# Rearranging the first 80 microseconds of a two-layer graph-attention kernel: wider loads of x, an earlier row of factors, gathers without a gate

## The reference

```
h   = relu(layernorm(x))              # per row
Wh  = h @ W                           # 8192 x 128
e   = leaky_relu(src[:, None] + dst[None, :], 0.2)   # src, dst = Wh @ a[:128], Wh @ a[128:]
att = softmax(where(adj > 0, e, -inf), axis=1)
```

## Time and profile before

| | us |
|---|---|
| runs (3) | 1973.93, 1978.59, 1979.74; median 1978.59 |
| the profiled execution | 1969.02, span of its trace 1967.1 |
| PE busy (span share) | 1906.6 (97%) |
| DVE, ACT, POOL busy | 1740.1 (88%), 1471.5 (75%), 1242.6 (63%) |
| first matmul of tile 0 | 82.13 |
| PE's longest stop after it | 130.55 to 135.67 |

### The profile page before, as it was taken

One profiled execution on the slowest core, in us unless ns is written; L12 is line 12 of the kernel. 1 busy time (PEld: TensorE's weight loads), 2 busy tenths in 40 slices (PEclk: granted clock), 3 DMA queues, 4 the chain that ended last, 5 costly groups with the idle time before them and its releaser, 6 DMA issues.

```text
span 1967.1 us, 39089 instructions
## 1 busy us (share of the span) xinstructions
PE 1906.6 (97%) x16858; PEld 1898.0 (96%) x16858; DVE 1740.1 (88%) x2023; ACT 1471.5 (75%) x1745; POOL 1242.6 (63%) x1010
## 2 busy tenths in 40 slices
PE   4789999999999999999999999999999999999998
PEld 3689999999999999999999999999999999999997
DVE  7888898998989899898969898998989899898985
ACT  4988897888889888898771877777788777778710
POOL 3675776767767575775640777767677676768600
PEclk9799999999999999999999999999999999999999
DMA  8999898899989788897990798888989788888900
GB/s 252 349 344 342 291 320 268 299 328 344 319 287 334 275 304 285 309 328 268 370 361 12 262 365 290 299 306 292 338 285 332 274 300 308 293 329 295 329 19 13
DMA packets 181381, 566.46 MB, mean 288 GB/s; under 512 B 18768, under 2 KB 49872, under 8 KB 179664
## 3 DMA queue, kind: packets, MB, share of 16 engines
q0 software_dynamic: 142848, 520.16, 74.9%
q1 hardware_dynamic: 33424, 41.36, 6.3%
q10 hardware_dynamic: 4928, 2.36, 0.5%
HBM read 548.01 MB, written 15.79 MB: 287 GB/s over the span
## 4 chain that ended last, share of the span: by engine, by line
PE 86%; DMA 5%; DVE 4%; ACT 2%; POOL 1%; issue 1%; SPq 0%; DVEq 0%; POOLq 0%
PE psum L766 84%; DMA arena<-in_adj_dram,piece_rows 4%; ACT arena L360 2%; PE psum L724 1%; DVE arena L1063 1%; POOL arena L350 1%; DVE arena L864 1%; DVE arena L378 1%; DMA arena<-x_mid 1%; PE psum L713 0%; DVE st L839 0%; DMA arena<-in_x_dram 0%; POOL piece_rows L396 0%; PE psum L691 0%; DVE h_all L885 0%
## 5 line engine op out<-in xcount | busy, mean ns | idle before, releaser
L766 PE MATMUL psum<-h_all,arena 128*128 128x129 f32 x16384 | 1841.6, 275 | 10.1 <-DVE arena L1063 10.0
L766 PEld LDWEIGHTS psum<-h_all,arena 128*128 128x128 f32 x16384 | 1836.4, 192 | 13.0 <-DVE arena L1063 10.3
L350 POOL DMA_INDIRECT arena<-in_adj_dram,piece_rows x992 | 1233.2, 1243 | 623.7 <-ACT arena L360 434.0
L360 ACT ACTIVATE arena<-arena,half_step 128x1024 uint8<-128x1024 int32 x992 | 1370.5, 1440 | 287.2 <-DMA arena<-in_adj_dram,piece_rows 156.5
L1063 DVE SCALAR_TENSOR_TENSOR arena<-arena,sd_col 128x1024 f32<-128x1024 f32 x512 | 641.2, 1277 | 103.1 <-PE psum L766 98.4
L1063 DVE SCALAR_TENSOR_TENSOR arena<-arena,rho_col 128x1024 f32<-128x1024 f32 x448 | 563.5, 1278 | 69.3 <-PE psum L766 66.3
L378 DVE STREAM_TRANSPOSE arena<-arena 128x1024 f32<-128x1024 f32 x248 | 306.0, 1235 | 8.7 <-ACT arena L360 8.4
L360 ACT ACTIVATION_READ_ACCUMULATOR arena<-arena,half_step 128x1 f32 x512 | 92.5, 181 | 0.0
L1063 DVE SCALAR_TENSOR_TENSOR arena<-psum,rho_col,arena 128x1024 f32<-128x1024 f32 x64 | 79.1, 1267 | 6.8 <-PE psum L766 6.6
L724 PE MATMUL psum<-W_ext,arena 128*128 128x131 f32 x256 | 38.5, 313 | 13.5 <-DVE h_all L885 10.0
L724 PEld LDWEIGHTS psum<-W_ext,arena 128*128 128x128 f32 x256 | 36.3, 224 | 14.9 <-issue 10.6
(11 more groups left out here) (126 smaller groups left out, 195.1 us busy)
## 6 DMA issues: line engine op xcount, KB each, us to landing
arena<-in_adj_dram,piece_rows POOLq DMA_INDIRECT x992, 5.9
arena<-in_x_dram SPq DMA_DIRECT2D x48, 128.0 KB, 5.8
x_mid<-arena SPq DMA_DIRECT2D x8, 512.0 KB, 6.9
edgesT<-arena SPq DMA_DIRECT2D x4, 1024.0 KB, 9.1
arena<-edgesT SPq DMA_DIRECT2D x4, 1024.0 KB, 16.8
arena<-x_mid SPq DMA_DIRECT2D x8, 512.0 KB, 6.6
out_dram<-arena SPq DMA_DIRECT2D x28, 128.0 KB, 11.3
h_mid<-arena SPq DMA_DIRECT2D x6, 512.0 KB, 3.0
```

The costliest lines, as they stand in the source:

```text
L350: pool.indirect_dma_start(adj_in[n % NA], None, adj_pieces, bass.IndirectOffsetOnAxis(ap=piece_rows[:, column:column + 1], axis=0))\
L360: nc.scalar.activation(pack_bytes[h][:, k, a], adj_in[n % NA], ACT.Sign, bias=half_step[:, 0:1], accum_out=into).then_inc(masked, 1)
L766: last = nc.tensor.matmul(acc_tile(g, k), wTs[m % RING][:, k * P:(k + 1) * P], h_all[:, j, 0:FZ], start=(j == 0 and k % 2 == 0), stop=(j = ...
```

## The change

- x is loaded in 16 DMAs of 256 KB with runs of 4 KB. A partition then holds 8 consecutive rows, and the order that the rest of the kernel wants is restored where the transposed z is copied out of PSUM: four instructions of 128 x 256 with a strided PSUM read replace each one of 128 x 1024.
- Layer 0's exponents are shifted by the maximum over the first eighth of the columns, known after part 0, instead of over all. Highest, lowest and invalid are still computed, within group 0's loop.
- `first_r` (the r of the first 8 tiles) runs on ACT ahead of mask 14; DVE limits it, PE transposes it, and it goes through DRAM to `r_row`; `diagonals` and `spread_r` are gone.
- POOL no longer waits for x.
- The copies of h stand between the normalisings, one part later than before.

```diff
+FIRST_R = 14
             indices(0, 0, G)
-            pool.wait_ge(x_loaded[XP // 2 - 1], 16 * BK)
             for n in range(len(PASSES) * PIECES):
                 load_piece(pool, n)
-                if n == 2:
-                    pool.wait_ge(x_loaded[XP - 1], 16 * BK)
...
-        def load_x(eng, i, which):
-            for q, block in quarters(x, i)[2 * which:2 * which + 2]:
-                eng.dma_start(x_all[q, part_of(0, i), :], block).then_inc(x_loaded[i], 16)
+        def load_x(eng, pair, which):
+            two = x_all[:, 2 * pair * TP:(2 * pair + 2) * TP, :].rearrange("p (i u) f -> p i (u f)", i=2)
+            for b in (2 * which, 2 * which + 1):
+                eng.dma_start(two[b * BP:(b + 1) * BP], eight_rows(pair, b)).then_inc(x_loaded[pair], 16)
...
+            load_weights(1, W1, a1)
+            sp.wait_ge(z_turned[0], 1)
+            store_r(0, 0, G)
+            load_r(4, slice(0, GW))
+            store_r(1, G, T)
             load_r(0, slice(GW, 3 * GW))
             load_xr(0)
...
-                nc.scalar.activation(zTs[i % 2], zT_ps(0, i), ACT.Relu).then_inc(zT_ready[0], 1)
+                for b in range(BK):
+                    last = nc.scalar.activation(ordered_rows(zTs[i % 2], b), turned_rows(i, b), ACT.Relu)
+                last.then_inc(zT_ready[0], 1)
...
+                if i == FIRST_R:
+                    act.wait_ge(ref_ready, 1)
+                    first_r(0, G)
                 if i == PIECES - 2:
                     exps()
                 mask_piece(act, i)
...
             for i in range(XP):
                 if i + 1 < XP:
                     turn_z(0, i + 1)
+                if i == 1:
+                    turn_extremes(0, first_spread_ps)
+                    spread_extremes(0, first_spread_ps)
+                    pe.wait_ge(ref_ready, 1)
+                if i == 3:
+                    turn_r(0, r_col, first_rT_ps, 0, G)
+                    pe.wait_ge(rows_ready, 1)
                 products(0, i)
-            turn_extremes(0)
-            spread_extremes(0)
-            spread_r()
...
             keep_h(0)
+            for step in range(3):
+                find_reference(0, step)
+            normalise(0, 4, x_part(4), x_part(4))
             keep_h(1)
-            normalise(0, 4, x_part(4), x_part(4))
+            normalise(0, 5, x_part(5), x_part(5))
             keep_h(2)
-            normalise(0, 5, x_part(5), x_part(5))
-            keep_h(3)
+            limit_r(r_col, r_ready, 1, 0, G)
             dve.wait_ge(zT_ready[0], 4)
             keep_zT(4)
+            keep_rows(0, first_rT_ps, G)
             normalise(0, 6, x_part(6), x_part(6))
+            keep_h(3)
             keep_zT(5)
             normalise(0, 7, x_part(7), x_part(7))
             keep_h(4)
             keep_zT(6)
+            turn_edges(dve, 0, 0, 0)
+            turn_edges(dve, 0, 0, 1)
             keep_h(5)
             keep_zT(7)
-            for s in range(SUBS):
-                turn_edges(dve, 0, 0, s)
+            turn_edges(dve, 0, 0, 2)
+            turn_edges(dve, 0, 0, 3)
             keep_h(6)
             keep_h(7)
-            extreme_values()
-            diagonals()
+            dve.wait_ge(h_kept[0], 2 * XP)
+            keep_sd(G, T).then_inc(first_sd_kept, 2)
             dve.wait_ge(exps_ready, 1)
             fold(0)
             turn_edges(dve, 0, 1, 0)
-            dve.wait_ge(r_spread, 1)
+            dve.wait_ge(r_loaded[4], 16)
```

More of the change, by code:

```diff
@@ L208, in kernel_program @@
         set_up = sem(p + "vector_set_up")
-        x_loaded = [sem(p + f"x_loaded{i}") for i in range(XP)]
+        x_loaded = [sem(p + f"x_loaded{i}") for i in range(XP // 2)]
         w_loaded = [sem(p + f"w_loaded{i}") for i in range(2)]
@@ L238, in kernel_program @@
         r_stored = sem(p + "r_stored")
-        r_loaded = [sem(p + f"r_loaded{i}") for i in range(4)]
+        r_loaded = [sem(p + f"r_loaded{i}") for i in range(5)]
         ref_ready = sem(p + "ref_ready")
@@ L297, in quarters, with eight_rows @@
             return [(slice(b * BP, (b + 1) * BP), four[c, b, :, t:t + TP, :]) for b in range(BK)]
+        def eight_rows(pair, b):
+            c, q = divmod(2 * pair, XP // COLS)
+            parts = x.rearrange("(c b q m u) f -> c b m q (u f)", c=COLS, b=BK, q=XP // COLS, m=BP)
+            return parts[c, b, :, q:q + 2]
         def part_of(layer, i):
@@ L476, in sync_fast @@
             load_weights(0, W0, a0)
[L477 to L481, removed]
+            for pair in range(XP // 2):
+                load_x(sp, pair, 0)
+            load_weights(1, W1, a1)
[3 more added lines that the diff above has]
+            store_r(1, G, T)
             load_r(0, slice(GW, 3 * GW))
@@ L575, in keep_first_h @@
                     into = tiles(ye)[:, half * TP // 2:(half + 1) * TP // 2, :]
[L576 removed]
+                    nc.scalar.activation(into, h_ps(0, half)[:, :, 0:F], ACT.Identity).then_inc(h_kept[1], 1)
             def keep_h(i):
                 if i == 1:
[L580 removed]
+                    act.wait_ge(ref_ready, 2)
                     act.wait_ge(sd_kept, 2)
@@ L593, in keep_h @@
                         into = tiles(ye)[:, t, :] if i < READY else h_all[:, b, 0:F]
-                        last = nc.scalar.activation(into, h_ps(1, i, half)[:, t - half * TP // 2, 0:F], ACT.Identity,
+                        last = nc.scalar.activation(into, h_ps(i, half)[:, t - half * TP // 2, 0:F], ACT.Identity,
                                                     scale=D_next[:, b:b + 1])
@@ L637, in scalar_fast @@
             zT_at = {3: 0, 4: 1, 7: 2, 8: 3}
-            for i in range(XP):
-                load_x(act, i, 1)
+            for pair in range(XP // 2):
+                load_x(act, pair, 1)
             act.wait_ge(set_up, 1)
@@ L879, in keep_zT @@
                     dve.wait_ge(h_done[0], 2 * (i - 1))
-                nc.vector.tensor_scalar(zTs[i % 2], zT_ps(0, i), 0.0, None, ALU.max).then_inc(zT_ready[0], 1)
+                for b in range(BK):
+                    last = nc.vector.tensor_scalar(ordered_rows(zTs[i % 2], b), turned_rows(i, b), 0.0, None, ALU.max)
+                last.then_inc(zT_ready[0], 1)
             def keep_h(i):
@@ L1145, in between @@
                     fold_next(g, j)
-                    if g == 0 and j == 0:
-                        keep_rows(0, rT_ps, T)
-                    if g == 0 and j == 2:
+                    if g == 0 and j == 1:
+                        limit_r(r_col, r_ready, 2, G, T)
+                    if g == 0 and j == 8:
+                        keep_rows(1, rT_ps, T - G)
+                    if g == 0 and j == 9:
+                        first_extremes()
+                    if g == 0 and j == 15:
+                        reduce_extremes(1, spread_ps)
+                    if g == 0 and j == 21:
+                        keep_extremes(1).then_inc(low_known, 1)
+                        dve.wait_ge(low_known, 1)
                         judge(0)
```

180 lines of the change are left out of this document (94 added, 86 removed).

## The result

The changed kernel is slower: median 1995.53 us (1991.48 to 1999.47, 6 runs) against 1976.72 (1967.47 to 1979.74, 6 runs of the kernel before), a ratio of 1.0094 with a 95% interval of 1.0074 to 1.0114. That is 18.8 us; the prediction had 4.5 and a range that ended at 1989.5.

The account below looks back on a forecast made before the run. Mask 63 was taken to bound the kernel through PE's stop before tile 26: 2.9 us later at mask 42 plus 1.6 for moved loads, 4.5 in all, 1983.1 us; own range 1981.5 to 1985, over the cases 1973 to 1989.5.

Parts of the forecast that it names:

- Mask 63 decides tile 26: Before tile 26, PE's stop ends when ACT's mask 63 is done; forecast 4.5 us later.
- PE's arrival: Looser limit on tile 26: first matmul at 87.1 plus 48.4 and 1 gives 136.5, earlier than 140.2, so not deciding.
- What follows moves along as a whole: After 135.67 us ACT, POOL and DVE are paced by PE, so the rest shifts with tile 26.
- DVE's idleness ahead of limiting r: DVE reaches the first limiting of r at 47.6 and stands 6.7 us, r being ready at 54.25.
- From r to the last copy of h: Stretch from r ready at 54.25 to the last copy of h at 80.25: 26.0 us, against 23.4 before.
- The strided copies: Four-instruction copies of z out of PSUM: 1.6 us on ACT and 1.65 on DVE, upper bounds 2.4 and 2.7.
- the rival that doubles them: Strided PSUM reads of z cost double per column: 9.5 us slower, 1988; chance 0.2, with late x in it.
- SP's half of the first two pairs lands near 11.5 ... 16.1: Start: three queues share 383 GB/s evenly, x lands near 11.5 and the first half's variance is ready at 16.1.
- The 15.5 taken: Time taken for the first half's variance, between 14.4 and 16.1; a gain of 0.7 us.
- the prediction's own sign of being wrong: At the start: a variance of the first half later than 17 us would show the forecast wrong.
- the refill behind the iotas: Loads of r and x, moved near 107 us, partly meet gathers restarting after the iotas: 0 to 3 us, taken 1.6.

Follow-up runs that it names:

- e11: Kernel before with the eight iotas moved ahead of the first gather; 1969.23 against 1977.27 us, ratio 0.9963.
- e5: Kernel before with only x's loading changed to wide pairs and strided copies of z, POOL still gated by x; 1978.52 against 1977.81 us, ratio 1.0003.
- e4: Kernel before with only POOL's two waits for x taken out; ratio 1.0075 to the kernel before, slower chip.
- e9: Changed kernel with group 0's r copied to PSUM and its tiles formed from there; 1987.72 us, ratio 1.0063 to the kernel before.
- e3: Changed kernel with x for the residual loaded ahead of the second store of r and the load of its rest; ratio 0.9884 to the kernel before, slower chip.
- e7: Changed kernel with the 1 MB load of r held back until half of group 0 is formed; ratio 1.0114 to the kernel before.
- e10: Kernel before with group 0's r copied from PSUM to SBUF and its tiles formed from there; 1980.75 against 1977.27 us, ratio 1.0017.
- e2: Changed kernel with the first r computed ahead of mask 8 instead of 14; ratio 0.9904 to the kernel before, slower chip.
- e8: Changed kernel with ACT's copy of z part 3 ahead of mask 13 instead of mask 8; 1992.08 us, ratio 1.0075 to the kernel before.
- second profile of the changed kernel: Changed kernel run again unedited, on a chip where the kernel before takes 1977.8 us; 1997.94 us, ratio 1.0101.
- e1: Changed kernel with POOL's two waits for x put back; ratio 0.9862 to the kernel before, slower chip.
- e15: Changed kernel with POOL gated by x again, same kernel as e1; ratio 0.9939 to the kernel before, slower chip.
- e18: Changed kernel with POOL gated by x, same kernel as e1 and e15; ratio 0.9892 to the kernel before, slower chip.
- e12: Changed kernel gated by x, z part 3 and first r ahead of mask 13, group 0's r in PSUM, iotas early; 1971.77 us, ratio 0.9972.
- e14: Changed kernel gated by x, group 0's r in PSUM, z part 3 ahead of mask 13; ratio 0.9967 to the kernel before, slower chip.
- e13: Changed kernel gated by x, with group 0's r in PSUM; ratio 0.9955 to the kernel before, slower chip.
- e16: e12 with the copy of r to PSUM moved ahead of DVE's wait for the exponents; ratio 1.0036 to the kernel before, slower chip.
- e17: Same kernel as e14, run once more; 2106.3 us against 2125.5 for the kernel before, slower chip.

## Why the prediction was wrong

**Right.** Mask 63 decides tile 26, not PE's arrival (DVE waits 11.78 us for it); e11 shows it from the other side. What follows moves along as a whole, but for the place near 1040 us. DVE's idleness ahead of limiting r, forecast 6.7 us, was 7.12. From r to the last copy of h: forecast 26.0, measured 25.4 to 25.5. From there to mask 30: 1.35 and 1.2. From the start of mask 30 to the end of mask 42: 18.5 us for 17.9, with one wait of 0.44. From the first copy of h to mask 30 the chain took 45.73 us for a forecast 45.76; that is partly luck, since r came 0.6 us later on this scale and the stretches behind it were 0.65 shorter. The strided copies took 1.21 on ACT and 1.40 on DVE, less than the 1.6 and 1.65 taken and 0.19 more on either engine than the one contiguous instruction had; the rival that doubles them is refuted by e5 and by these rows.

**Wrong, first: the landing of x.** The step "SP's half of the first two pairs lands near 11.5 ... 16.1" was meant as the upper bound. The second pair was whole at 16.65 and the variance ready at 21.09. The mechanism, three queues sharing, was right; the rate and the start were not. The rate was 306 GB/s at 11 to 14 us and 260 to 311 around it, not 383, and SP's queue, counted from its issue at 2.16, had moved 0.07 MB by 5 us. (The stated shares, a third of 383 GB/s for 1.05 MB from 2.16, give 10.4 and not 11.5; no row covers the difference.) The second weights, issued behind x on SP, landed late too, a wait that the sum did not have. Together the first copy of h came at 43.18 for a forecast 35.84, 7.3 us. The 15.5 taken leaned in part on the earlier trace rows, where the gathers had only just begun; e4 shows that they do share. A variance later than 17 was the prediction's own sign of being wrong.

**Wrong, second: a term that was missing.** The sum treated the row of r as the same work in another place. It read `r_of` for its timing and not for where the operand lies. With r in SBUF, forming takes DVE no longer (1.27 to 1.28) but can hold up POOL's gathers where DVE runs without gaps. I forecast 0 to 3 us for the refill behind the iotas, by the loads of r and x, and took 1.6. Tile 26 came 15.8 us later than forecast (156.0 for 140.2), of which 7.9 were already there at the end of mask 42; the other 7.9 are here. From there to tile 26 the changed kernel took 48.6 us, the kernel before 39.0 and e9 39.7. e3 and e7 refute the loads one by one, and e9, which keeps both loads, gives 8.8 us back at tile 26. The Trainium skill (SBUF — State Buffer, Who interferes with whom) says that DVE and GpSimd share a pair of SBUF ports under an exclusive lock, and that a DVE instruction with two SBUF inputs contends with a GpSimd one that reads SBUF. The traces agree as to when: up to 4.25 us for a gather beside forming with both inputs in SBUF, 0.94 in e9 with one in PSUM. That the port is the reason is the skill's account; the runs show only where the operand lay and what the gathers took. They show too that the hold is not certain: e10's gather of 0.94 us stands beside the same three operations.

**Right stall, wrong reading.** Of two idle stretches that follow from one another I charged DVE's. e2 removed it and gained 2 us at mask 30; e8 removed ACT's, and DVE's with it, and gained 7. Between the first copy of h and mask 8 the changed kernel takes 10.5 us and the kernel before 6.4. Of these 4.1 the reference's round trip ahead of products 1 is 3.1 (3.91 us from copy to product against 0.85); the product, the turn and the copy that follow are slower by the rest. ACT, in order, stands at z part 3 with its masks behind.

**The account.** From 135.67 to 155.89, in the second profile of the changed kernel: 6.9 us up to the first copy of h (gathers at once 5.5 by e1, pairs 1.6 by e5); 4.0 at z part 3; 1.5 to mask 30; then 4.4 won up to the start of mask 48, with the loads of r and x moved away; and 12.2 lost from there to the end of mask 63. Of the last, 8.0 are the SBUF forming by e9 (38.4 us, against 30.3 in e9 and 26.2 in the kernel before). The other 4 are the hole behind the iotas, which stand 7.8 us in POOL's queue: with ACT free of other waits it shows in full, and it takes back what the moved loads had won. This split was read from the rows; no run has the changed kernel with the iotas moved and nothing else. At tile 26 the three edits give 1.9 to 4.7 us (gating), 6.9 (e8) and 8.8 (e9), together 17.6 to 20.4 of the 20.2. In whole times e8 gave 5.9 us and e9 7.5 to 9.7; for gating there are only profiles.

## What to carry to other kernels

When an operand moves between PSUM and SBUF, look at what runs beside the instruction that reads it, and not only at its duration: DVE's 1.28 us stayed, and three gathers on POOL went from 0.94 to between 3.2 and 4.25. It costs only where the gathers decide, as behind the iotas here. When two engines each stand idle behind one cause, undo them in turn and see which moves the deciding event: DVE's alone gave 2 us at mask 30, ACT's gave 7. And look for fixed work in a queue that can stand where that queue waits anyway: eight iotas moved into a wait of 11 us gave 7 to 8 us.

## What the runs showed of the hardware that was not expected

**A gate that looks idle was worth its wait.** Six gathers issued at 3.4 to 10.7 us made the variance 2 to 3.3 us and the first copy of h 4.3 to 5.8 us later than in e1, e15 and e18, and gave ACT nothing: its first mask, behind the square root of the variance, started at 21.26, and in e1 at 21.18.

**Near 1040 us the time varies from run to run.** PE's wait for ACT's copy of z part 7 of layer 1 was 0.2 us in the profile of before but 5.76 in that of the changed kernel, 7.77 in its second, 5.86 in e7 and 6.3 to 9.2 in those of e5, e8, e9, e10, e11 and e12. The row of e5, whose time is that of the kernel before:

```profile
1022.48 3.53 PE L738 MATMUL psum<-W_ext,arena 128*128 128x131 f32 x16 [6.33 <-ACT arena L567]
```

In the changed kernel's second profile one gather just ahead of that place took 9.10 us on POOL, beside a DVE that forms seven tiles from SBUF without gaps:

```profile
1021.03 8.45 DVE L1092 SCALAR_TENSOR_TENSOR arena<-arena,rho_col 128x1024 f32<-128x1024 f32 x7
...
1021.20 9.10 POOL L363 DMA_INDIRECT arena<-in_adj_dram,piece_rows  x1 [0.30 <-issue]
```

One gather there took 7.5 to 9.1 us in each of these profiles. In that of the kernel before DVE forms the same seven tiles without gaps, and the gathers pass:

```profile
1000.62 8.58 DVE L1063 SCALAR_TENSOR_TENSOR arena<-arena,rho_col 128x1024 f32<-128x1024 f32 x7
...
1000.89 1.83 POOL L350 DMA_INDIRECT arena<-in_adj_dram,piece_rows  x1 [0.34 <-ACT arena L360]
...
1003.02 0.94 POOL L350 DMA_INDIRECT arena<-in_adj_dram,piece_rows  x1 [0.31 <-issue]
```

So the same work held one gather for 9.10 us in one execution and none for over 2 us in another, and from tile 475 to the end of layer 0 the two executions differ by 9.8 us. That the held gather makes PE's wait is read from the traces and was not tested. Elsewhere a hold over several operations is rare: of the 992 gathers of the kernel before 386 took over 1.3 us, and one over 2.1 (4.27, at 357 us, in a group formed from SBUF).

**On two chips PE seemed to run short of instructions.** There rows like this (e14) repeat about every 1.43 us for some stretches, mostly three or four matmuls and then a gap that nothing in the profile released:

```profile
123.99 1.10 PE L794 MATMUL psum<-h_all,arena 128*128 128x129 f32 x4 [0.44 <-issue]
```

Why is open, and so is why variants of the changed kernel came out at 0.986 to 1.004 of the kernel before there. One pattern stands out: PE took 49.4 to 50.4 us for tiles 0 to 25 in e1, e2, e3, e15 and e18, which form group 0 from SBUF, and 57.4 to 75.8 in e4, e13, e14, e16 and e17, which form it from PSUM and whose gathers come faster. No run tests this. That the changed kernel is slower holds for the chips of normal speed.
